# Moving both output products and splitting the layer-norm roots of a 25-chunk mix stage interleaved with a graph attention

## The reference, cut to what matters

```
xn = layernorm(x)
x1 = x + gnn(xn, edges) + mix(xn)        # the change lies in mix
y  = x1 + ffn(layernorm(x1))             # 8 experts, three products each

gnn: h = xn @ W_src; e = leaky(a_src[src] + a_dst[dst]); alpha = softmax of e per dst
     out[dst] += alpha * h[src]          # then layer norm and PReLU

mix: q, k, v = xn @ Wq, xn @ Wk, xn @ Wv
     Q = elu(q) + 1; K = elu(k) + 1; KV = sum over rows of K * v, per head
     msg = (Q . KV) / (Q . sum K) ; msg = layernorm(msg @ Wm) * g1 + b1
     h = relu(concat(xn, msg) @ W1) @ W2
     mix = xn + layernorm(h) * g2 + b2
```

## Time and profile before

| | |
|---|---|
| median of the runs | 4496.52 us |
| the profiled execution | 4500.52 us, its span 4498.6 us |
| PE busy | 4114.9 us, 91% of the span |
| DVE busy | 3540.2 us, 79% |
| ACT busy | 2321.1 us, 52% |
| POOL busy | 1750.7 us, 39% |
| mean granted TensorE clock | 0.96 |

### The profile page before, as it was taken

How to read it: one execution, slowest core, us unless ns; L and a number is a source line. 1 busy time by engine, 2 the same in 40 slices (tenths; PEclk the granted TensorE clock), 3 DMA queues, 4 the chain that set the end, 5 groups by cost and what they waited for, 6 DMA issues and landing times. The chain is left out here.

```text
span 4498.6 us, 82317 instructions
## 1 busy us (share of the span) xinstructions
PE 4114.9 (91%) x23402; PEld 3317.4 (74%) x23403; DVE 3540.2 (79%) x8844; ACT 2321.1 (52%) x4488; POOL 1750.7 (39%) x1798
## 2 busy tenths in 40 slices
PE   8975999998998999999998866999999999999999
PEld 7864666666666666666666645888888888888888
DVE  8865787777777778778777877788787887878787
ACT  5642444444444444444443424666666666666666
POOL 2227777777777777777776740000000000000000
PEclk9987999999999999999999987999999999999999
DMA  6545666666666666666666652000000000100000
GB/s 203 185 152 142 174 186 170 168 186 170 167 184 176 167 179 182 166 177 182 169 176 167 168 141 66 29 15 28 21 21 28 14 28 14 28 28 14 28 14 19
DMA packets 344854, 510.24 MB, mean 113 GB/s; under 512 B 43528, under 2 KB 268416, under 8 KB 344704
## 3 DMA queue, kind: packets, MB, share of 16 engines
q0 software_dynamic: 84480, 234.40, 21.7%
q1 hardware_dynamic: 260224, 274.20, 19.0%
HBM read 325.55 MB, written 182.89 MB: 113 GB/s over the span
## 5 line engine op out<-in xcount | busy, mean ns | idle before, releaser
L873 POOL DMA_INDIRECT acc<-h_tab,strips x1760 | 1685.8, 958 | 674.3 <-issue 553.8
L1386 PE MATMUL ps<-acc 128*128 128x260 f32 x3520 | 1022.3, 418 | 32.6 <-DVE acc L1008 26.6
L1386 PEld LDWEIGHTS ps<-acc 128*128 128x128 f32 x3520 | 641.5, 202 | 107.2 <-DVE acc L1008 17.9
L1008 DVE SCALAR_TENSOR_TENSOR acc<-acc,strips,ps 128x260 f32<-128x260 f32 x880 | 419.1, 476 | 210.0 <-PE ps L1386 203.9
L1922 ACT ACTIVATE exp<-ps,bn 128x512 f32<-128x512 f32 (+1 forms) x400 | 310.1, 775 | 452.4 <-PE ps L1989 448.2
L994 DVE TENSOR_TENSOR acc<-acc,ps 128x1024 f32<-128x1024 f32 x440 | 532.5, 1210 | 2.0
L1987 PE MATMUL ps<-w_hi,b_hi 128*128 128x256 f32 x1568 | 444.9, 284 | 1.2 <-DVE exp L1825 1.2
L1989 PE MATMUL ps<-w_hi,b_lo 128*128 128x256 f32 x1568 | 443.6, 283 | 0.0
L1988 PE MATMUL ps<-w_lo,b_hi 128*128 128x256 f32 x1568 | 443.5, 283 | 0.0
L1200 ACT ACTIVATE strips<-ps 128x512 bf16<-128x512 bf16 x440 | 261.9, 595 | 237.2 <-PE ps L1361 233.3
L1833 DVE TENSOR_TENSOR a_lo<-exp,a_hi 128x512 fp32r<-128x512 f32 (+1 forms) x400 | 258.8, 679 | 144.4 <-ACT a_hi L1924 133.3
(11 more groups left out here) (275 smaller groups left out, 8377.2 us busy)
## 6 DMA issues: line engine op xcount, KB each, us to landing
side_tab<-acc SPq DMA_DIRECT2D x440, 260.0 KB
acc<-h_tab,strips POOLq DMA_INDIRECT x1760
acc<-xnt_tab SPq DMA_DIRECT2D x50, 512.0 KB, 5.6
h_tab<-proj SPq DMA_DIRECT2D x25, 520.0 KB, 6.8
exp<-side_tab SPq DMA_DIRECT2D x100, 130.0 KB, 2.3
proj<-in_x SPq DMA_DIRECT2D x25, 512.0 KB, 5.4
base_tab<-proj SPq DMA_DIRECT2D x25, 512.0 KB, 3.2
xnt_tab<-proj SPq DMA_DIRECT2D x25, 512.0 KB, 6.2
```

What stands on the lines that cost most here:

```text
L873: pool.indirect_dma_start(G[s][:, b * GU + u], None, h_tab, bass.IndirectOffsetOnAxis(REC[s][:, b * GU + u, 0:1], 0)).then_inc(g_in[s], 16)
L1008: nc.vector.scalar_tensor_tensor(A[:, k % (2 * BS)], A[:, (k - 1) % (2 * BS) if k else 2 * BS], smt[s][:, k:k + 1], ps[k % BANKS][:, 0:MW] ...
L1386: ins = nc.tensor.matmul(ps[k % BANKS][:, 0:MW], S32[b % 2][:, i * DU + u], G[s][:, b * GU + i * DU + u], start=u == 0, stop=u == DU - 1)
```

## The change

The change touches the order of the mix only, in five places, and no arithmetic:

- PE's outputs of chunk n-1 stand in slots 9 and 10 instead of 2 and 9, and ACT's copies of them with them (in slot 10 behind `normalize` of the merge). Both wait for both copies of the merge of chunk n, or for the first output's copy. The denominators' wait on the output's copy goes.
- DVE's statistics of the output stand in slots 10 and 11 instead of 3 and 10.
- `deviations` handles one layer norm at a time: for the merge in slot 9, for the output in slot 12, both behind the second add, each with a chain of twelve root steps of its own.
- `normalize` waits for its own chain.
- ACT's second `attended` copy stands at the end of slot 6 instead of in the middle of slot 7.

```
-                def deviations(n):
-                    cur, prev = chunks(n)
-                    if cur:
-                        ln_st[0].wait(dve, n)
-                    if prev:
-                        ln_st[1].wait(dve, n - 1)
+                def deviations(c, i):
+                    ln_st[i].wait(dve, c)
                     pass_on(dve, "dve")
-                    both = slice(0 if cur else 1, 2 if prev else 1)
-                    for i in range(both.start, both.stop):
-                        for t in range(CH):
-                            ins = nc.vector.bn_aggr(bmv[:, i, t], bstats[:, i, t])
-                    ins.then_inc(ln_ag.sem, 1)
-                    ln_ag.wait(dve, n)
-                    rsqrt(dve, ln_rs, n, 0, brs[:, both], bmv[:, both, :, 1], btv[:, both], btt[:, both], LN_EPS)
...
+                    for t in range(CH):
+                        ins = nc.vector.bn_aggr(bmv[:, i, t], bstats[:, i, t])
+                    ins.then_inc(ln_ch[i].sem, 1)
+                    ln_ch[i].wait(dve, c, 1)
+                    rsqrt(dve, ln_ch[i], c, 1, brs[:, i], bmv[:, i, :, 1], btv[:, i], btt[:, i], LN_EPS)
...
 DVE mix_between
-                    if prev and i == 3:
-                        statistics(n - 1, 1, 0)
                     if cur and i in (8, 9):
                         statistics(n, 0, i - 8)
-                    if prev and i == 10:
-                        statistics(n - 1, 1, 1)
-                    if (cur or prev) and i == 10:
-                        deviations(n)
+                    if prev and i in (10, 11):
+                        statistics(n - 1, 1, i - 10)
 DVE mix_after
+                    if cur and i == 9:
+                        deviations(n, 0)
+                    if prev and i == 12:
+                        deviations(n - 1, 1)
 ACT normalize
-                    ln_nb.wait(act, c + i)
+                    ln_ch[i].wait(act, c)
 ACT mix_first
-                    if cur and i == 7:
-                        attended(n, 1)
 ACT mix_last
-                    if prev and i in (2, 9):
-                        o_copy(n - 1, i // 8)
...
                     if cur and i == 10:
                         normalize(n, 0)
+                    if prev and i in (9, 10):
+                        o_copy(n - 1, i - 9)
 ACT turn, at the end of the block
                         if b == 6 and q2 is not None:
                             destinations(act, q2, 1 - sq)
+                        if here and s == 0 and b == 6 and chunks(n)[0]:
+                            attended(n, 1)
 PE denominators
-                    o_cp.wait(pe, c - 1, 1)
 PE output
                     if h:
                         o_cp.wait(pe, c, 1)
-                    if cur and h:
+                    elif cur:
                         m_cp.wait(pe, n)
-                    elif cur:
-                        q_act.wait(pe, n)
 PE mix_mid
-                    if prev and i in (2, 9):
-                        output(n - 1, i // 8, n, cur)
+                    if prev and i in (9, 10):
+                        output(n - 1, i - 9, n, cur)
```

More of the change, by code:

```diff
@@ L318, in build @@
         ln_st = [stage(f"{v}_st", 2) for v in ("m", "o")]
-        ln_ag, ln_rs, ln_nb = stage("ln_ag"), stage("ln_rs", RSQ), stage("ln_nb")
+        ln_ch = [stage(f"ln_ch{i}", RSQ + 2) for i in range(2)]
         o_norm, o_g, o_base = stage("o_norm"), stage("o_g", 2), stage("o_base", 2)
@@ L1038, in statistics @@
                     ins.then_inc(ln_st[i].sem, 1)
-                def deviations(n):
-                    cur, prev = chunks(n)
-                    if cur:
-                        ln_st[0].wait(dve, n)
-                    if prev:
-                        ln_st[1].wait(dve, n - 1)
-                    pass_on(dve, "dve")
-                    both = slice(0 if cur else 1, 2 if prev else 1)
-                    for i in range(both.start, both.stop):
-                        for t in range(CH):
-                            ins = nc.vector.bn_aggr(bmv[:, i, t], bstats[:, i, t])
-                    ins.then_inc(ln_ag.sem, 1)
-                    ln_ag.wait(dve, n)
-                    rsqrt(dve, ln_rs, n, 0, brs[:, both], bmv[:, both, :, 1], btv[:, both], btt[:, both], LN_EPS)
-                    nc.vector.scalar_tensor_tensor(nb[:, both], bmv[:, both, :, 0], -1.0, brs[:, both], ALU.mult, ALU.mult
-                                                   ).then_inc(ln_nb.sem, 1)
+                def deviations(c, i):
+                    ln_st[i].wait(dve, c)
+                    pass_on(dve, "dve")
+                    for t in range(CH):
[3 more added lines that the diff above has]
+                    rsqrt(dve, ln_ch[i], c, 1, brs[:, i], bmv[:, i, :, 1], btv[:, i], btt[:, i], LN_EPS)
+                    nc.vector.scalar_tensor_tensor(nb[:, i], bmv[:, i, :, 0], -1.0, brs[:, i], ALU.mult, ALU.mult
+                                                   ).then_inc(ln_ch[i].sem, 1)
                 def o_scale(c, h):
```

## The result

The changed kernel takes 4384.8 us, the median of 4 runs (4382.39 to 4386.13), against 4498.1 (4494.46 to 4500.02) for the kernel before in the same comparison: a ratio of 0.9746, 95% interval 0.9734 to 0.9757. The forecast was 4373, its range 4362 to 4425. The profiled execution has a span of 4380.5 us, 118.1 less than before.

The account below looks back on a forecast made before the run. PE bounds the kernel, POOL's gathers five per cent behind. PE's terms give 6.5 us a chunk, 160 us, but gathers cap the gain at 123.7: 4500.5 - 123.7 = 4376.8, less 4.0 for the median, 4373 us; range 4362 to 4425.

Parts of the forecast that it names:

- What bounds the kernel, and that the gathers would take over: Second stage: PE sets 85.33 us a chunk; after the change POOL's gathers, 1.2555 us each, limit the gain to 123.7 us.
- Slots 11 and 12: Without the 3.09 us stall and at 2.4 GHz, they take 10.05 us instead of 16.08: 6.0 us less.
- The first output leaves slot 2: Slots 2 and 3 lose 3.45 us of PE work; DVE gains 2.5 us, PE waits about 1.4 us in slot 5.
- The second attended copy, 1.46 us: Moved to slot 6, it ends the merge's 1.72 us wait; slot 8 gains at most 1.46 us, then limited by its message.
- The sum for PE: Per chunk 4.0 - 3.45 + 6.0 = 6.5 us less, a chunk of 78.8 us; 160 us over 24.5 chunks.
- The signs: Expected: chunk about 80.3 us, ACT waiting for gathers, no low clock, last gather near 2523 us, DVE about 65 us busier.
- the sign named for a DVE that slows POOL: In POOL's gathers: a pitch above 1.26 us without waits would mean that DVE slows POOL.
- The low clock: Rival: PE's idle time still brings a low stretch each chunk; 4401 us, or 4425 with a 1 us stall; chance 0.22.
- The rival of no change, 4495: Slots 2 to 8 keep their length and slot 11's stall returns in slot 10 with low clock: about 4495 us; chance 0.06.
- DVE's slowing of the gathers: Rival: the added chain's three first steps delay POOL's gather issue 0.66 us a chunk, 17 us in all: 4390 us; chance 0.12.
- The slower case: Rival: PE waits out DVE's chains in slots 9 and 12, 2.3 us a chunk slower: 4554 us; chance 0.04.
- The moved outputs: Outputs in slots 9 and 10: PE pays 3.45 us more in slot 10, DVE gains 2.5 us in slots 2 and 3.

Follow-up runs that it names:

- The split alone: Kernel before with only separate root chains for the merge (slot 9) and the output (slot 12); outputs and second attended copy unmoved: 4382.04 us, ratio 0.9742.
- the copy alone: Kernel before with only ACT's second attended copy moved from slot 7 to the end of slot 6: 4510.05 us, ratio 1.0029.
- the bank shifted: Changed kernel with the three aggregation banks shifted by one in odd groups: 4397.22 us, ratio 0.9776.
- the late copy: Changed kernel with ACT's second attended copy put back in slot 7: 4383.29 us, ratio 0.9747.
- The runs with 30 gathers: 30 gathers a group instead of 32 from the third group on: kernel before 4488.16 us, changed kernel 4373.5, the split alone 4336.27, the late copy 4346.1.

## Why the prediction was right, and where it was not

**What bounds the kernel, and that the gathers would take over.** Right, and it is what kept the forecast near. PE's stall and low clock set 85.33 us (taking two gathers out of each group of the kernel before changed nothing in mid-stage), and the last gather moved by 114.4 us where I had 123.7. The pitch was mis-sized: I took 1.2555 us from a stretch of the kernel before, and it was 1.2614, which is 10.4 us over 1759 gathers. The first gather starts 1.1 us earlier than before and the work behind the last one is 3.7 us shorter, so the profiled executions differ by 5.6 us (4376.8 forecast, 4382.4 measured). The rest of the 11.8 us to the median of 4384.8 is which execution was profiled: 4.0 us above the median before, 2.4 below it after. I took the pitch for a constant of POOL's. It isn't: where DVE's two-input instructions fall on the gathers it goes to 1.2689, and with two of them changed to 1.2562.

**Slots 11 and 12.** Right: 6.0 us less were forecast, 6.2 came (16.08 to 9.87). The split alone brings it, as the second run shows. (By the slot starts, the two windows of the earlier trace rows lie in slots 11 and 12, not 12 and 13.)

**The first output leaves slot 2.** DVE's gain of 2.5 us is there: slots 2 to 7 got 2.64 us shorter, and the copy alone didn't shorten them. The short waits of PE in slot 5 are 0.53 and 0.22 us (0.43 and 0.22 before) rather than 1.4; PE's idle time gathered in front of slot 8 instead.

**The second attended copy, 1.46 us.** This step failed. I wrote that the message of slot 8 was "what is late next". It isn't: the first aggregation of a group waits for the last add of the group before, since both use bank 0, a wait that stands in `aggregate` and that I left out. The row that shows it is this one of DVE in the kernel before, the last add of slot 7:

```profile
1017.89 0.48 DVE L1008 SCALAR_TENSOR_TENSOR acc<-acc,strips,ps 128x260 f32<-128x260 f32 x1
```

It ends at 1018.37 and slot 8 began at 1018.43: there was no room of 1.46 us, only of 0.06. The profile named ACT as the one waited for, because PE had stood in front of the merge. The copy alone is worth less than nothing (4510), and with the bank shifted, PE's wait becomes the 0.61 us for the message that I had in mind.

**The sum for PE.** 78.8 us were forecast. The terms as measured are 2.64 for slots 2 to 7, -3.19 for slot 10 and 6.21 for slots 11 and 12, 5.7 us in all: 79.6, which is the length of the chunks with full clock. The chunks with a low stretch take 81.33, so the mean of 80.8 is, by coincidence, also the pace of 64 gathers (80.7). This is why neither shows a wait for the other: PE alone needs 80.78 us a chunk, the gathers at 1.2614 us need 80.7. Which of the two holds the changed kernel can't be said from its own trace; taking PE's loss away (the late copy) and taking gathers away (30 a group) each leave it nearly where it was, as with two equal bounds. The 11 us of the latter are about the 10 that the kernel before gains too from shorter last groups. For the forecast this was luck: the sum for PE was 2 us a chunk too low, and PE's real pace only happened to be that of the gathers.

**The signs.** POOL's wait for PE went to nothing, the last gather came near 2523, and the waits in slots 7 and 11 went, as said. Three signs failed: ACT didn't wait for the gathers in mid-stage, since PE was no faster than they; the low clock stayed in 14 places; and DVE got 43.6 us busier (3583.8 against 3540.2), not 65. The pitch of 1.2614 without waits is the sign named for a DVE that slows POOL, and it was right.

**The rivals.** The low clock came back in a milder form, 1.7 us in about two chunks of three instead of 2.6 in each, and behind a stall of 1.9 us that I had put at 0.4. I had argued that 1.72 us of idle time didn't bring it; 1.9 us did. With the gathers as a second bound it cost the changed kernel nothing that can be measured. The rival of no change, 4495, doesn't follow from its own terms: 3.45 - 1.46 is 2.0 us more a chunk, which is 49 us slower. It didn't come. DVE's slowing of the gathers is real too, but not by the instructions that I had named. While the first new chain runs (its roots from 1154.70 to 1157.3), the gathers go on as before:

```profile
1154.24 0.95 POOL L873 DMA_INDIRECT acc<-h_tab,strips  x1 [0.30 <-issue]
1155.49 0.95 POOL L873 DMA_INDIRECT acc<-h_tab,strips  x1 [0.30 <-issue]
1156.74 0.95 POOL L873 DMA_INDIRECT acc<-h_tab,strips  x1 [0.30 <-issue]
```

The slower case did not come: the chain in slot 9 is hidden under the output product, as was said, and DVE's second chain costs nothing in slot 12: slots 12 and 13 begin without a wait.

**The moved outputs** are a part without a use, as is the moved copy. I had priced them at 3.45 - 2.5 = 0.95 us of loss for PE, and put that loss inside a sum that looked good. The runs with 30 gathers give 0.5 us, with the late copy on both sides of the comparison.

## What to carry to other kernels

Before counting on a wait that goes away, look for every semaphore that the next instruction of that engine waits on, in the code: the trace names only the one that came last, and another may end 0.06 us before it. When a stage has two bounds within a few per cent, price the second one first, since it caps the gain whatever the first one gives; leaving some of its work out shows how much is hidden behind it. And price each part of a change by itself: here one of three gave everything, and another, which only moved a stall, gave a loss that the second bound covered. A second bound need not be a constant either: here the moment at which DVE's instructions ran moved POOL's pace.

## What was not expected of the hardware

An indirect DMA on POOL takes 0.946 us, and up to 1.43 when it starts while DVE runs a 128x512 instruction with both inputs in SBUF; the same DVE instruction with one input from PSUM doesn't do this, nor do the 0.16 us steps of a root chain. Over 1760 gathers it made 22 us between two kernels with the same order. The other is the clock. With PE alone, a wait of 1.7 us in front of the merge in each chunk left the clock at 2.4 GHz (one low stretch from 560 to 2320 us), and a wait of 1.9 us behind it brought 15 low stretches of 3.4 us. Whether the place decides or the 0.2 us of length was not tried, nor why only two chunks of three have one.
